# Second half of the late passes in five, two and one destination tiles instead of six and two

## The reference

```python
def _gat(x, adj, W_heads, a1, a2, W_out, b_out):          # layer 0
    Wh = jnp.einsum('nf,hfd->hnd', x, W_heads)
    s1 = jnp.einsum('hnd,hd->hn', Wh, a1)
    s2 = jnp.einsum('hnd,hd->hn', Wh, a2)
    e = s1[:, :, None] + s2[:, None, :]
    e = jnp.where(e > 0, e, ALPHA * e)
    e = jnp.where(adj[None, :, :] > 0, e, NEG)
    att = jax.nn.softmax(e, axis=-1)
    hp = jax.nn.elu(jnp.einsum('hnm,hmd->hnd', att, Wh))
    feat = jnp.transpose(hp, (1, 0, 2)).reshape(N, NHEADS * NHID)
    return feat @ W_out + b_out
...
h = jnp.maximum(_layernorm(x, axis=-1), 0.0)
x = x + _L0_gnn_ref(h, adj, ...)                           # 8 heads, ELU, projection
h = jnp.maximum(_layernorm(x, axis=-1), 0.0)
x = x + _L1_gnn_ref(h, adj, ...)                           # one head, exact GELU
h = jnp.maximum(_layernorm(x, axis=-1), 0.0)
x = x + _L2_gnn_ref(h, adj, ...)                           # one head, ELU
h = jnp.maximum(_layernorm(x, axis=-1), 0.0)
x = x + _L3_gnn_ref(h, adj, ...)                           # one head, ELU
```

## Time and profile before

| | us |
|---|---|
| median of 3 runs | 754.32 |
| profiled execution | 754.51 |
| its span in the trace | 752.8 |
| TensorE busy | 742.0 (99%) |
| VectorE busy | 624.3 (83%) |
| ScalarE busy | 326.6 (43%) |
| granted TensorE clock, mean | 0.999 |

### The profile page before, as it was taken

One profiled execution on the slowest core, in us unless ns is written; L12 is line 12 of the kernel. 1 busy time (PEld: TensorE's weight loads), 2 busy tenths in 40 slices (PEclk: granted clock), 3 DMA queues, 4 the chain that ended last, 5 costly groups with the idle time before them and its releaser, 6 DMA issues.

```text
span 752.8 us, 16085 instructions
## 1 busy us (share of the span) xinstructions
PE 742.0 (99%) x6505; PEld 731.8 (97%) x6505; DVE 624.3 (83%) x1048; ACT 326.6 (43%) x884; POOL 16.6 (2%) x38
## 2 busy tenths in 40 slices
PE   9999999999999999999999999999999999999997
PEld 8899999999999999999999999999889989998997
DVE  5998879797797967979787797968788969898986
ACT  4978432462443435144253424534450352636230
POOL 4000000000000000000000000000000000000000
PEclk9999999999999999999999999999999999999999
DMA  9991000000000000000000000000000000000001
GB/s 292 377 394 60 30 29 1 28 0 28 28 0 28 0 28 26 2 28 0 28 2 25 28 0 28 0 0 1 2 2 1 1 1 2 1 1 1 2 28 30
DMA packets 13874, 29.39 MB, mean 39 GB/s; under 512 B 1296, under 2 KB 7568, under 8 KB 13840
## 3 DMA queue, kind: packets, MB, share of 16 engines
q1 hardware_dynamic: 11152, 20.00, 7.5%
q0 software_dynamic: 2688, 8.92, 3.4%
HBM read 27.80 MB, written 1.11 MB: 38 GB/s over the span
## 4 chain that ended last, share of the span: by engine, by line
PE 94%; ACT 3%; DVE 2%; issue 1%; POOL 0%; POOLq 0%; DVEq 0%
PE acc L461 55%; PE acc L486 26%; PE side L585 3%; PE side L409 3%; ACT adjT L723 1%; PE acc L430 1%; PE acc L538 1%; ACT V L756 1%; PE acc L388 1%; PE side L549 1%; PE side L525 0%; PE side L511 0%; PE side L440 0%; DVE stats L1431 0%; ACT xn L947 0%
## 5 line engine op out<-in xcount | busy, mean ns | idle before, releaser
L461 PE MATMUL acc<-V,probs 128*128 128x129 f32 x3840 | 436.7, 275 | 1.8 <-DVE probs L1230 1.6
L461 PEld LDWEIGHTS acc<-V,probs 128*128 128x128 f32 x3840 | 432.6, 192 | 2.7 <-DVE V L1175 1.8
L1233 DVE SCALAR_TENSOR_TENSOR probs<-rho,t_now,adjT 128x1024 f32<-128x1024 f32 x238 | 290.0, 1277 | 10.4 <-PE acc L461 8.5
L1324 DVE SCALAR_TENSOR_TENSOR probs<-rho,t_now,adjT 128x768 f32<-128x768 f32 (+3 forms) x182 | 147.3, 869 | 13.3 <-PE acc L486 10.5
L819 ACT ACTIVATE hpT<-rows 32x256 f32<-32x256 f32 x224 | 92.8, 414 | 66.6 <-DVE rows L1270 64.2
L486 PE MATMUL acc<-stage,probs 128*128 128x129 f32 x1024 | 115.9, 275 | 0.2
L486 PEld LDWEIGHTS acc<-stage,probs 128*128 128x128 f32 x1024 | 115.0, 192 | 0.6 <-issue 0.6
L486 PE MATMUL acc<-V,probs 128*128 128x129 f32 x768 | 89.4, 275 | 0.1
L486 PEld LDWEIGHTS acc<-V,probs 128*128 128x128 f32 x768 | 87.4, 192 | 0.3 <-issue 0.3
L804 ACT ACTIVATE fill<-mean_now,empty 128x128 f32<-128x128 f32 x120 | 36.7, 397 | 92.1 <-DVE den L1246 92.1
L1278 DVE TENSOR_TENSOR X<-X,side 128x512 f32<-128x512 f32 x28 | 19.3, 688 | 63.6 <-PE side L585 63.6
(11 more groups left out here) (207 smaller groups left out, 406.1 us busy)
## 6 DMA issues: line engine op xcount, KB each, us to landing
stage<-in_adj_t_dram SPq DMA_DIRECT2D x24, 512.0 KB, 8.2
rho<-rho_dram POOLq DMA_DIRECT2D x15, 512.0 KB, 3.8
hpT<-in_adj_t_dram SPq DMA_DIRECT2D x4, 512.0 KB, 8.8
xn<-in_adj_t_dram SPq DMA_DIRECT2D x4, 512.0 KB, 9.2
X<-in_x_dram SPq DMA_DIRECT2D x2, 512.0 KB, 4.6
W0t<-in_W_t_dram SPq DMA_DIRECT2D x1, 512.0 KB, 5.3
W<-in_L_gnn_W_heads_dram SPq DMA_DIRECT2D x1, 512.0 KB, 6.6
Wout<-in_L_gnn_W_out_dram POOLq DMA_DIRECT2D x1, 512.0 KB, 9.4
```

What stands on the lines that cost most here:

```text
L461: last = nc.tensor.matmul(group(c, k), probs[:, j % RING, k * P:(k + 1) * P], V[:, j, :], start=(j == 0 and k % PER_BANK == 0), stop=(j == ...
L1233: nc.vector.scalar_tensor_tensor(probs[:, j % RING, :], rho[:, c * CH:(c + 1) * CH], t_now[:, j:j + 1], adjT[:, j, c * CH:(c + 1) * CH], A ...
L1324: return nc.vector.scalar_tensor_tensor(slot_of(n, p, j)[:, first:end], rho[:, at + first:at + end], t_now[:, j:j + 1], adjT[:, j, at + fi ...
```

## The change

The second half is cut into p = 1 (five tiles), p = 2 (two) and p = 3 (one); `tiles_of`, numbering and waits follow. The group of the last tile lies in bank 1 behind p = 1's two groups there (`late_group`), and since the first matmul of a bank clears it, p = 3 waits until bank 1's groups have been read (`last_bank_read`). Probability tiles of p = 2 are now 384 wide and hold the columns of p = 2 and of p = 3; two share a slot, and p = 3 makes none of its own. VectorE makes 14 of them ahead of p = 1's denominators and two after. Three tiles (13 to 15) are multiplied before their scale is known (`RAW = 13`), and their scale is taken together after the last tile's statistics. In n = 2's scale three Newton steps (nine instructions) become one step of higher order and one Newton step (seven). The three `WARM_ROWS` fillers of n = 1 are gone. Transposes of the five (and for n = 1 the projection of the two) move into the p = 3 unit, the products of the first eight into the p = 2 unit. Scores of k = 1 are made in two halves. ScalarE's lists are reordered to suit; for n = 2 its table load stands ahead of the copy of the last tile. The output goes out in four transfers instead of three.

```diff
-    WARM_START, WARM_ROWS, WARM_HOLE = 20, 3, 3
+    WARM_START, WARM_HOLE = 20, 3
-    PARTS = (((0, 4), (4, 4)), ((0, 4), (4, 2)), ((6, 2),))
-    FIRST, CHUNKS, TWO = (0, 2, 4), 5, 14
-    NORM_DVE = ((0, 0), (1, 1), (2,))
+    PARTS = (((0, 4), (4, 4)), ((0, 3), (3, 2)), ((5, 2),), ((7, 1),))
+    FIRST, CHUNKS, RAW = (0, 2, 4, 5), 6, 13
+    RAWS, PACK = NT - RAW, 2
+    NORM_DVE = ((0, 0), (1, 1), (2,), (1,))
...
+        def late_group(c, k):
+
+            bank, slot = (k // PER_BANK, k % PER_BANK) if c == 0 or k < 5 else (2, k - 5) if k < 7 else (1, 2)
+            return acc[:, c, bank, slot * VW:slot * VW + VW]
...
+            def last_bank_read(n, p, i):
+
+                if n == 2:
+                    pe.wait_ge(late_exp, chunk_no(2, p, i))
+                else:
+                    pe.wait_ge(late_rows, rows_no(n, p, i))
...
-                    else:
-                        pe.wait_ge(probs_ready, tile_no(n, p, j) + 1)
+                    elif p < 3:
+                        pe.wait_ge(probs_ready, probs_no(n, p, j) + 1)
+                    elif j == 0:
+                        last_bank_read(n + 1, 1, 1)
...
-                             (13, 0): lambda: transpose_normed(1, 0, 0, x_written, chunk_no(1, 0, 0)),
-                             (14, 1): lambda: transpose_normed(1, 0, 1, x_written, chunk_no(1, 0, 1)),
-                             **scores_of_half(1, 15)})
-            late_unit(0, 2, {(7, 0): lambda: transpose_rows(1, 0, hT_ready, 1),
-                             (8, 0): lambda: transpose_rows(1, 1, hT_ready, 2),
-                             (9, 0): lambda: project_rows(1, 0),
-                             (10, 1): lambda: project_rows(1, 1)})
+                             (15, 0): lambda: transpose_normed(1, 0, 0, x_written, chunk_no(1, 0, 0))})
+            late_unit(0, 2, {(0, 1): lambda: transpose_normed(1, 0, 1, x_written, chunk_no(1, 0, 1)),
+                             (3, 0): lambda: late_wh(1, 0, 0),
+                             (5, 0): lambda: late_wh(1, 0, 1),
+                             (7, 0): lambda: transpose_rows(1, 0, hT_ready, 1),
+                             (9, 0): lambda: transpose_rows(1, 1, hT_ready, 2),
+                             (10, 0): lambda: project_rows(1, 0),
+                             (12, 0): lambda: project_rows(1, 1)})
+            late_unit(0, 3, {(6, 1): lambda: transpose_normed(1, 1, 0, x_written, chunk_no(1, 1, 0)),
+                             (8, 1): lambda: transpose_normed(1, 1, 1, x_written, chunk_no(1, 1, 1)),
+                             (10, 1): lambda: transpose_rows(2, 0, wh_kept, 1),
+                             (14, 1): lambda: project_rows(2, 0)})
...
+                    if n == 1:
+                        late_unit(n, 1, {(14, 0): half[0], (15, 0): half[1]})
+                        late_unit(n, 2, {(1, 0): half[2], (3, 0): half[3]})
+                        late_unit(n, 3, {(6, 1): five[0], (8, 1): five[1],
+                                         (13, 1): lambda: transpose_normed(m, 2, 0, x_written, chunk_no(m, 2, 0))})
+                    else:
+                        late_unit(n, 1, {(15, 0): half[0]})
+                        late_unit(n, 2, {(0, 1): half[1], (4, 0): half[2], (6, 0): half[3]})
+                        late_unit(n, 3, {(8, 1): five[0], (10, 1): five[1]})
...
-                    for it in range(3):
-                        link(nc.vector.scalar_tensor_tensor(s, g, -0.5, g, ALU.mult, ALU.mult))
-                        link(nc.vector.tensor_tensor(s, s, v, ALU.mult))
-                        link(nc.vector.scalar_tensor_tensor(y, s, 1.5, g, ALU.add, ALU.mult))
-                        g = y
+                    link(nc.vector.scalar_tensor_tensor(s, g, 1.0, g, ALU.mult, ALU.mult))
+                    link(nc.vector.tensor_tensor(s, s, v, ALU.mult))
+                    link(nc.vector.scalar_tensor_tensor(s, s, -10.0 / 3.0, s, ALU.add, ALU.mult))
+                    link(nc.vector.scalar_tensor_tensor(y, s, 5.0, g, ALU.add, ALU.mult))
+                    link(nc.vector.scalar_tensor_tensor(s, y, -0.5 * 0.375 ** 3, y, ALU.mult, ALU.mult))
+                    link(nc.vector.tensor_tensor(s, s, v, ALU.mult))
+                    link(nc.vector.scalar_tensor_tensor(y, s, 1.5 * 0.375, y, ALU.add, ALU.mult))
...
-            tiles(0, 2, 0, 16)
+            tiles(0, 2, 0, 14)
             late_denominators(1, 1)
             late_divide(1, 1, 0)
             late_divide(1, 1, 1)
             late_elu_rows(1, 0)
             late_elu_rows(1, 1)
+            tiles(0, 2, 14, 16)
```

278 lines of the change are left out of this document (152 added, 126 removed).

## The result

| | before, us | after, us |
|---|---|---|
| median of 11 runs | 754.32 | 756.01 |
| ratio after / before (95%) | | 1.0023 (1.0013 to 1.0032) |
| span of the profiled execution | 752.8 | 754.3 |
| TensorE busy | 742.0 | 740.3 |
| VectorE busy | 624.3 | 626.8 |

The changed kernel is 1.7 us slower, a difference of 0.2% that the interval keeps away from zero; by the measure of 2% it is no change. The prediction said 755.7. One of the eleven executions of the kernel before took 1556.9 us; it does not move the median, and no trace shows what it was.

A forecast was written before the change was run, and what follows sets the result against it. TensorE, busy 99% of the span, was taken as the bound, through its instructions and waits. 1.8 - 0.5 + 0.3 - 0.6 + 0.35 = +1.35 us on 754.51 gave 755.9, as a median 755.7; range +0.3 to +3 us.

The forecast's parts named there:

- handover 1: Last aggregation matmul of a layer to the next layer's first, first of three: first maximum 1.8 us later, bounds -0.9, +2.8.
- handover 2: Second handover between layers: no TensorE stall, shorter way to the maximum, -0.5 us, bounds -1.3 and +0.8.
- handover 3: Third handover between layers: stalls of 0.75 and 0.6 us, shorter way to the maximum, +0.3 us, bounds -1.1 and +1.3.
- end: Behind the last unit: division, exponential and additions of one tile, not two; last addition 0.6 us sooner.
- sum over three rows: Layers 2 and 3: one tiny matmul more in each, with its share of a switch 0.17 us each, +0.35 together.
- the first two rivals: 384-column tile near 0.396 us: 751.6, chance 0.22; at 0.60 us, VectorE later still: 758.7, chance 0.12.
- VectorE late at the denominators: Handovers 1 to 3: denominators of the five 3.6, 2.1 and 3.5 us behind TensorE's last matmul on them.
- Waits in the last units: TensorE's waits inside the last units: 2.6 us in handover 1, none in 2, 1.35 in 3.
- From the last unit's end to the maximum: Path behind the last unit in handovers 1 to 3: 6.8, 4.5 and 4.2 us.
- the cover holds: Rival: 384-column tile near 0.396 us, VectorE 1.9 us sooner, no transpose waits, -2.75 us to 751.6; chance 0.22.
- nothing comes of it: Rival: stalls in the units take what the shorter chain gives, only the end's gain remains, 754.0; chance 0.10.
- the fourth: Rival: in a new wait the clock falls to 1.2 GHz, slower by over 2%; chance 0.01.

The follow-up runs named there:

- the run with 256 columns: Changed kernel, with VectorE making only 256 of 384 columns in layer 2's last 16 probability tiles (work left out, timing only): 756.21 us in one execution.
- rebuilt handover 1: Changed kernel, first pass only: VectorE's tiles, scale and norm and TensorE's products, transposes and projections reordered; 753.44 us, 0.9991 of the kernel before.
- the repaired kernel: Changed kernel with rebuilt handover 1 plus layer 2's transposes of the five after steps 13 and 15: 753.15 us, 0.9983 of the kernel before.

## Why the prediction was right

The number came out (755.7 for 756.01), and each of its five terms within 0.35 us. By its own steps:

| term | predicted | measured |
|---|---|---|
| handover 1 | +1.8 | +2.14 |
| handover 2 | -0.5 | -0.53 |
| handover 3, without the sum over three rows | +0.3 | +0.51 |
| end | -0.6 | -0.8 |
| sum over three rows, layers 2 and 3 | +0.35 | +0.44 |
| sum | +1.35 | +1.76 |

For handover 3 and the end, 0.22 of the sum over three rows is taken out of each stretch. With the 0.27 that the unchanged part ahead took less in this execution, 1.76 becomes the 1.5 of the two spans. The medians differ by 1.69, so the change was put 0.3 to 0.4 us too low. It would have been more without the end, which gained more than forecast: the last addition ends 0.51 sooner once the sum over three rows is taken out, for 0.6, but what stands behind it is 0.28 shorter, which I had put at nothing.

**The width of the tiles** was a guess between 0.396 and 0.93 for 384 columns, taken from the line: 0.53. It measured 0.53. This one value decided between the forecast and the first two rivals, which needed 0.396 or 0.60.

**VectorE late at the denominators**, 3.6, 2.1 and 3.5 us: measured 3.57, 2.11 and 3.43. The times at which TensorE sums the five follow from counts of instructions, and counted from the start of their pass they held to 0.1 in the first two handovers and to 0.2 in the third, where the sum over three rows comes on top.

**Waits in the last units**, 2.6, none and 1.35: measured 2.74, none and 1.40. They were worked out from how long the same chain took before, with one tile more or less, against TensorE's own count. In handover 1 the end of the last unit was forecast 40.19 us behind p1 (544.4 less 504.21), and came at 40.25.

**From the last unit's end to the maximum**, 6.8, 4.5 and 4.2: measured 7.04, 4.46 and 4.37. This is the step that was mis-sized: of 0.34 missing in handover 1, 0.24 stand here, and 0.17 of the 0.21 in handover 3. For the last transpose, its copy by ScalarE and the matmul behind I gave 0.46 us, and the rows show 0.64 (549.59 to 550.23). Another 0.21 is missing in the steps from the unit's end to that transpose, and 0.15 came back behind it (1.00 us to the maximum for 1.15).

**The cause in handover 3 was told wrongly, though its size was right.** "The forecast rests on this", I wrote of the 14 tiles ahead of the denominators. In handover 1 that holds for the first wait alone; the second stays with eight tiles ahead as with 16. For handover 3 it is refuted: eight, 14 or 16 ahead of them give the same waits. It is the whole of VectorE's work ahead of the normalised rows that counts. My sum held since it counted the two tiles behind the denominators too, and not because the cause was the right one. And "nil over a layer", of 640 plus 384 columns against 768 plus 256, is right as a sum (85.2 us for 59 and 64 tiles against 85.4 for 60 and 64) and wrong as a price: the saving fell into waits, the cost onto the path, 1.45 us by the run with 256 columns. Without it handover 3 would be shorter than before by about 0.7.

**The fillers** I took as 0.67 us of work that is gone. Returned, they cost 0.48, since part of their time falls into a wait that is there anyway (0.56 us ahead of the transpose of the last rows).

**The rivals.** That the cover holds (751.6) fell with the 0.53. That nothing comes of it (754.0) fell too: the waits in handovers 1 and 3 took more than the shorter chain gave. The rebuilt handover 1 shows what was right in the first rival: the gain is there for a better order, 0.43 of the 0.9 that it bounded (both without the fillers). Its condition alone would not have brought it: with the denominators 3.2 us sooner, the second wait of handover 1 stood as before. Of the fourth, a fall of the clock, the trace shows nothing in the late part: 1.00 through waits of up to 1.70 us and with the fillers gone. The Trainium skill (TensorE: Matmul & The Clock Gate, Why this matters for your kernels) warns that idling between bursts of matmuls brings half rate back; the late part of these traces, in which the changed kernel's longest wait is 1.70 us, shows no such fall.

## What to carry to other kernels

When columns move from one pass to another, price them by place and not by sum: a saving where the engine waits anyway is worth nothing, and the same columns in the stretch that a handover waits for cost most of their time (here 1.45 of 2.1 us). Before moving a dependent step ahead of independent work on an in-order engine, compare the two arrival times: the step belongs behind as much independent work as is left, up to the moment when its input is ready. And once its wait is gone, look at whether the producer has idle time left, since about that much can still be won. When a change has several parts, price those apart that do not need the others: here the shorter scale and the missing fillers hold most of what the repaired kernel gains.

## What the hardware showed beyond expectation

The cost of a probability tile on VectorE is a line in the columns: 477, 611, 748, 878, 1014 and 1279 ns for 256, 384, 512, 640, 768 and 1024 columns, 1.04 ns a column and 0.21 us fixed. Back to back, the next starts about 0.08 us sooner than that. The instruction reads two tensors and one column of scalars (`t_now`). The same operation on two tensors with a constant in place of that column is shorter, 692 ns against 748 for 512 columns:

```profile
L1470 DVE SCALAR_TENSOR_TENSOR X<-rows,X 128x512 f32<-128x512 f32 x4 | 2.8, 692 | 0.1
```

For 256 and 384 columns it is 425 and 558 ns, so the difference is 52 to 56 ns whatever the width. That the column of scalars makes it was not tried apart from the other operands. The Trainium skill (VectorE: DVE Perf Modes, TRN2 errata) gives (N + 151) / 0.96 ns for an fp32 `tensor_tensor` of N columns, by which an estimate is 691 ns for 512. The rows with a constant agree (692), and the probability tiles lie above it.

The part ahead of p1 has two lengths with the same code: 503.65 to 504.25 us in seven of the profiles and the kernel before, 505.5 to 505.6 in three. All three show a lower granted clock between 12 and 16 us. The rebuilt handover 1, columns as above:

```profile
8.00:12.00 4.00, 3.22 (x28) 3.23 (x29) 3.28 (x21) 2.97 (x11) 4.00 (x9) 0.95 1.12 350
12.00:16.00 4.00, 4.00 (x23) 4.00 (x22) 1.81 (x5) 2.66 (x5) 1.26 (x2) 0.63 1.04 355
```

TensorE got through 23 instructions between 12 and 16 us; the changed kernel's profile has 35 at a clock of 1.00. From 16 to 20 us the clock is 1.00 again. A mean of 0.63 means that it ran at 1.2 GHz, the lower level, for most of the stretch. It had waited just ahead, for a load. The changed kernel waited there too, and kept its clock. First the rebuilt handover 1, then the changed kernel:

```profile
8.78 1.05 PE L631 MATMUL acc<-a_sb,W0t 128*128 128x2 f32 x8 [0.94 <-DMA W0t<-in_W_t_dram]
...
8.83 1.05 PE L631 MATMUL acc<-a_sb,W0t 128*128 128x2 f32 x8 [0.79 <-DMA W0t<-in_W_t_dram]
```

The three profiles with the fall have the three longest of these waits, 0.94, 1.04 and 1.04 us. The other eight have 0.79, 0.56 or none. So the fall and the long wait go together in eleven profiles; that the wait makes the fall was not tried, and in the late part waits of 1.04 and 1.70 us bring none. The 1.6 us between the two lengths are about what the whole change costs (1.7), and stand in a part that it does not touch.
